# A third sum for the scatter-added expert blocks, and a loop unrolled by twelve

## The chip, the cores and the metric

The kernel runs on one core of one Trainium2 chip. A core has five engines with a queue of instructions each: TensorE (PE, matmuls; its weight loads are listed as PEld), VectorE (DVE), ScalarE (ACT), GpSimd (POOL) and SyncE (SP, which here issues DMAs). They run side by side and are tied together by semaphores. The metric is the device time of one execution in microseconds (us); lower is better.

## What is computed

One post-norm transformer layer in fp32 on 8 sequences of 512 tokens, width 256: attention with 16 heads, residual and layernorm; then a mixture of 16 experts of which each token takes 6, plus a shared expert, residual and layernorm.

```python
x = _layernorm(x + attn(x))                      # (8, 512, 256), causal
probs = softmax(xf @ gate_w.T); _, idx = top_k(probs + gate_b, 6)
cw = weights of the 6 chosen experts, 0 elsewhere
for each expert e:
    h = silu(xf @ W1.T + B1) * (xf @ W3.T + B3)
    y = y + cw[:, e:e+1] * (h @ W2.T + B2)       # each token gets 6 such terms
z = silu(xf @ ws1.T + bs1) * (xf @ ws3.T + bs3) @ ws2.T + bs2
out = _layernorm(x + y + z)
```

## The kernel before

The kernel works in three stages.

**Attention and routing (to about 530 us of the profile).** A loop over 8 sequences does attention, the first layernorm and the router. The normed tokens go to DRAM twice: as rows of `x1_d`, and, one copy for each chosen expert, by an indirect DMA of POOL into `xs_d`, where each expert's tokens stand together. Each row of `xs_d` carries its gates and its token number. At the end, tables say which expert each block of 128 rows belongs to.

**Blocks.** `BLOCKS` = 207 blocks of 128 rows go through their expert one after the other. For block k, SP loads the rows to `xb[k % 4]`; PE transposes them (L1029), ACT and DVE split them into a high and a low part (`xb_hi`, `xb_lo`), PE multiplies by the expert's first weights (bias L1038, product L1042), ACT and DVE make silu times gate (`hb`), PE transposes that (L1053), it is split again (`hb_hi`, `hb_lo`) and multiplied by the second weights (L1069). ACT weighs the result by the gate into `y_sb[k % 4]` (`weigh`, L1336), and POOL adds its 128 rows to a sum in DRAM by an indirect, accumulating DMA (`add_rows`, L2074). A token can be in any block, so two adds to the same sum must not be under way together. There are two sums: block k adds to `x1_d` where k is even and to `z_d` where it is odd, and waits on `added[k % 2]` until the add of block k - 2 has landed. `weigh` of block k waits for the add of block k - 4, whose `y_sb` buffer it overwrites, and the second product of block k + 2 waits for `y_out`, since PE has two PSUM banks for it.

The blocks are written out by `UNROLL` = 8: two turns straight (`LATE_TURNS`, in which the last four experts' weights still come in), 23 turns of a hardware loop, and a last one of 7. At the start of every turn PE reads the eight blocks' weight offsets from a table into registers, four to an instruction (L1079), and SP does the same for its rows.

**Shared expert and closing pass.** The shared expert runs in 48 tiles T (3 for each of 16 pieces of 256 tokens): PE `shared_up` (L781), ACT silu (`hidden`, L1297) and `h_hi`, DVE gate (L1799), low part `h_lo`, PE `shared_down` (L1010). 30 tiles run before the blocks and their results are stored to `z_d`; 18 run behind them. With the tiles from 36 on, the closing pass takes the 16 pieces m in the order `FINAL_ORDER`: SP loads `fin_x` from `x1_d` and `fin_z` from `z_d` (L720), POOL adds the two (`final_sum`, L2085, two pieces ahead), DVE adds the shared expert's result from PSUM for the last six pieces (L1862), takes the statistics (L1866, L1871), and after each of five groups of pieces POOL makes the inverse deviation (L2100), DVE the shift (L1883) and ACT normalizes (L1374). The L1862 of a piece frees the PSUM bank in which PE wants to start the next but one. Every engine's order here is the order in which the code is written: on POOL low part of tile T, inverse if due, sum of piece m + 2; on DVE gate of tile T, split of x1 if due, shift if due, statistics of piece m.

## Time and profile before

| | |
|---|---|
| device time, 3 runs | 1142.87 us median (1142.61 to 1143.4) |
| profiled execution | span 1184.2 us; no other time of it is recorded |
| blocks, third turn to last (666.88 to 1097.74 us) | 430.86 us for 184 blocks |
| last add to a sum issued | 1127.52 us |
| last matmul | about 1170.8 us |

| engine | busy us | share of the span |
|---|---|---|
| PE | 1050.3 | 89% |
| DVE | 754.6 | 64% |
| POOL | 736.1 | 62% |
| ACT | 672.2 | 57% |

In the timelines below a row has the start in us, the duration in us, engine, line and operation, result and operands, how many instructions were merged, and in brackets how long the engine had been idle before it and what ended that. "issue" is idle time in which the engine waited for nothing that the profile shows. Matmul ends are modelled.

### The profile page before, as it was taken

The numbers are of one execution on the slowest core, as the hardware profiler recorded it, in microseconds if no ns is written. First come the engines' busy times: TensorE is split into PE (matmuls) and PEld (weight loads), VectorE is DVE, ScalarE is ACT, GpSimd is POOL, SyncE is SP. The second block draws the span as 40 slices with busy tenths as digits, with TensorE's granted clock in tenths as the row PEclk, the third lists the DMA queues.
The fourth block names the chain that finished last, engine by engine and source line by source line (L and its number), as shares of the span: only waits on it lengthen the run. The fifth ranks groups of instructions, "written<-read, shape, count | busy, mean of one in ns | idle before, by whom it ended". The sixth has DMA issues, their size and how long they took to land.

```text
span 1184.2 us, 28306 instructions
## 1 busy us (share of the span) xinstructions
PE 1050.3 (89%) x8028; PEld 853.9 (72%) x8029; DVE 754.6 (64%) x2400; ACT 672.2 (57%) x1684; POOL 736.1 (62%) x668
## 2 busy tenths in 40 slices
PE   7899998989898987885297999999999999999974
PEld 4546555545465544575287899999999999999973
DVE  8777787868777777465265655555555555555456
ACT  3666666656566666543145655555555555555536
POOL 4224387877778788664403566666666666666666
PEclk8999999999999999687599999999999999999987
DMA  6713344444444455465426676777776666666684
GB/s 183 193 44 109 102 125 167 142 154 128 155 137 159 142 181 157 147 216 168 161 100 169 120 119 116 116 118 119 117 118 112 116 114 112 117 111 120 108 286 151
DMA packets 127036, 163.53 MB, mean 138 GB/s; under 512 B 18800, under 2 KB 107504, under 8 KB 126704
## 3 DMA queue, kind: packets, MB, share of 16 engines
q1 hardware_dynamic: 82240, 99.73, 29.7%
q0 software_dynamic: 39024, 54.29, 24.4%
q10 hardware_dynamic: 5696, 8.55, 2.2%
q8 instruction: 41, 0.67, 0.3%
q14 instruction: 35, 0.29, 0.1%
HBM read 65.36 MB, written 73.85 MB: 118 GB/s over the span
## 4 chain that ended last, share of the span: by engine, by line
PE 66%; DVE 12%; DMA 6%; ACT 4%; issue 4%; another core or an unknown queue 4%; POOL 1%; SPq 1%; ACTq 0%; DVEq 0%; POOLq 0%
PE psum L1042 15%; PE psum L1069 11%; PE psum L781 9%; PE psum L811 5%; PE psum L823 5%; PE psum L796 4%; PE psum L1029 4%; PE psum L1053 3%; DVE rowmax L1479 3%; PE psum L1038 3%; DMA z_d<-y_sb,tokens 2%; PE psum L798 2%; ACT probs L1142 2%; DMA xb<-xs_d 2%
## 5 line engine op out<-in xcount | busy, mean ns | idle before, releaser
L1142 ACT ACTIVATE probs<-psum 128x512 f32<-128x512 f32 (+2 forms) x384 | 187.0, 531 | 128.6 <-PE psum L811 114.0
L1479 DVE TENSOR_REDUCE rowmax<-psum 128x1 f32<-128x512 f32 (+3 forms) x352 | 212.7, 633 | 69.9 <-PE psum L798 62.8
L2000 POOL DMA_INDIRECT xs_d<-x1p,index x192 | 199.7, 1040 | 65.6 <-issue 43.2
L2074 POOL DMA_INDIRECT x_d<-y_sb,tokens x104 | 162.8, 1566 | 116.5 <-ACT y_sb L1336 90.4
L1818 DVE TENSOR_TENSOR xb_lo<-psum,xb_hi 128x256 fp32r<-128x256 f32 x207 | 87.7, 424 | 199.7 <-ACT xb_hi L1133 198.7
L2074 POOL DMA_INDIRECT z_d<-y_sb,tokens x103 | 160.8, 1561 | 86.7 <-ACT y_sb L1336 56.3
L1042 PE MATMUL psum<-we_hi_lo,xb_hi 128*128 x828 | 200.3, 323 | 0.0
L1336 ACT ACTIVATE y_sb<-psum,combine 128x256 f32<-128x256 f32 x207 | 98.3, 475 | 150.5 <-PE psum L1069 51.5
L1069 PE MATMUL psum<-we_hi_lo,hb_hi 88*128 (+1 forms) x828 | 174.2, 303 | 0.0
L796 PE MATMUL psum<-stack_k,stack_q 96*128 96x256 bf16 (+3 forms) x512 | 138.7, 310 | 11.6 <-issue 5.4
L1042 PEld LDWEIGHTS psum<-we_hi_lo,xb_hi 128*128 128x128 f32 x828 | 145.9, 189 | 0.0
L1942 POOL TENSOR_SCALAR_AFFINE_SELECT probs<-probs 128x512 f32<-128x512 f32 x128 | 85.7, 670 | 96.8 <-ACT probs L1142 93.8
L811 PE MATMUL psum<-stack_q,stack_k 99*128 99x256 bf16 (+3 forms) x512 | 118.6, 307 | 28.3 <-ACT probs L1142 16.9
L1042 PE MATMUL psum<-we_hi_lo,xb_lo 128*128 x414 | 134.1, 324 | 0.0
L1069 PEld LDWEIGHTS psum<-we_hi_lo,hb_hi 88*128 88x128 f32 (+1 forms) x828 | 125.6, 189 | 0.2 <-issue 0.2
L1069 PE MATMUL psum<-we_hi_lo,hb_lo 88*128 x414 | 116.2, 281 | 0.0
L823 PE MATMUL psum<-probs,values 128*32 128x512 f32 (+3 forms) x1024 | 95.0, 456 | 9.6 <-DVE attn L1556 7.2
L811 PEld LDWEIGHTS psum<-stack_q,stack_k 99*128 99x128 bf16 x512 | 40.4, 98 | 85.4 <-ACT probs L1142 49.9
L798 PE MATMUL psum<-causal,ident_bf 128*128 128x128 bf16 x512 | 101.2, 224 | 0.0
L1326 ACT ACTIVATE hb<-psum 128x176 f32<-128x176 f32 x207 | 65.7, 317 | 61.6 <-PE psum L1042 56.1
L781 PE MATMUL psum<-x1T,ws_hi_lo 128*128 128x256 f32 x576 | 86.2, 300 | 8.3 <-issue 6.3
L796 PEld LDWEIGHTS psum<-stack_k,stack_q 96*128 96x128 bf16 x512 | 50.4, 99 | 56.8 <-issue 27.4
(205 smaller groups left out, 2353.7 us busy)
## 6 DMA issues: line engine op xcount, KB each, us to landing
xb<-xs_d SPq DMA_DIRECT2D x207, 138.0 KB
stack_q<-q_h SPq DMA_DIRECT2D x48, 128.0 KB
stack_k<-k_h SPq DMA_DIRECT2D x45, 128.0 KB
w_raw<-in_we SPq DMA_DIRECT2D x9, 608.0 KB
xT_raw<-in_xT SPq DMA_DIRECT2D x9, 512.0 KB
stack_q<-q_m SPq DMA_DIRECT2D x32, 128.0 KB
stack_k<-k_m SPq DMA_DIRECT2D x32, 128.0 KB
x_res<-in_x SPq DMA_DIRECT2D x8, 512.0 KB
```

The source lines that it names most:

```text
L781: last = nc.tensor.matmul(dst, lhs(a, k), rhs(b, k), start=n == 0, stop=n == 3 * KD - 1)
L796: nc.tensor.matmul(dst, stack_q[par][0:STACK, head, qt * P:qt * P + P], stack_k[par][0:STACK, head, 0:width], start=True, stop=False)
L798: last = nc.tensor.matmul(dst[:, width - P:width], ident_bf[:], causal[:], start=False, stop=True)
L811: last = nc.tensor.matmul(st[f % ST_BANKS][:, i * width:(i + 1) * width], stack_k[par][0:STACK + SHIFT_ROWS, head, kt * P:kt * P + P], sta ...
L823: last = nc.tensor.matmul(ov[32 * j:32 * j + 32, kt * P:S], values[par][:, kt, GH * g + j, :], probs[kt][:, j, :], start=kt == 0, stop=kt ...
L1042: last = nc.tensor.matmul(uv, (xb_hi, xb_lo)[a][k % 2][:, d, :], w_flat[:, bass.ds(at + b * W_COLS + d * UP, UP)], start=False, stop=d == ...
L1069: last = nc.tensor.matmul(y, (hb_hi, hb_lo)[a][k % 2][0:rows, d, :], w_flat[0:rows, bass.ds(at + b * W_COLS + W2_AT + d * D, D)], start=d ...
L1142: nc.scalar.activation(probs[kt][:, heads[0]:heads[0] + n, :], st[f % ST_BANKS][:, 0:n * width].rearrange("p (h t) -> p h t", h=n), ACT.Ex ...
L1336: nc.scalar.activation(y_sb[k % 4][:], y_ps[k % 2][:, 0:D], ACT.Copy, scale=combine[:, k:k + 1]).then_inc(y_out, 1)
L1479: nc.vector.reduce_max(rowmax[gpar][:, heads[0]:heads[0] + n, qt], src, AX.X).then_inc(sm_free, 1)
L2000: nc.gpsimd.indirect_dma_start(out=xs_d[:, :], out_offset=bass.IndirectOffsetOnAxis(ap=index[tp][:, n:n + 1], axis=0), in_=x1p[tp][:, n // ...
L2074: nc.gpsimd.indirect_dma_start(out=(x1_d, z_d)[k % 2][:, :], out_offset=bass.IndirectOffsetOnAxis(ap=tokens[:, k:k + 1], axis=0), in_=y_sb ...
```

## The change

There is a third sum, `y_d`, in DRAM. It starts as zeros: at the head of each of the first seven turns of the attention loop SP writes a piece of up to 640 rows from a tile of zeros. Block k now adds to sum k % 3, and waits for the add of block k - 3. `weigh` still waits for the add of block k - 4, which is now the semaphore of another sum. The blocks are written out by 12: two turns straight (24 blocks), 15 of the loop, a last one of 3. In the closing pass SP loads a third tile `fin_y` for each piece, and DVE adds it to `fin_x` ahead of L1862 or the statistics.

```diff
-UNROLL = 8
+UNROLL = 12
+SUMS = 3
...
+            def set_third_sum(piece):
+                rows = y_d[Y_ROWS * piece:min(Y_ROWS * piece + Y_ROWS, T_ALL + P)]
+                sp.dma_start(rows.rearrange("(q p) d -> p q d", p=P),
+                             pad_block[:, 0:D].unsqueeze(1).to_broadcast([P, rows.shape[0] // P, D])).then_inc(y_set, 16)
...
+                if b < Y_PIECES:
+                    set_third_sum(b)
...
-            for n, src, dst in ((1, z_d, fin_z), (0, x1_d, fin_x)):
-                sp.wait_ge(added[n], 16 * ((BLOCKS + 1 - n) // 2))
+            for n, src, dst in ((0, x1_d, fin_x), (1, z_d, fin_z), (2, y_d, fin_y)):
+                sp.wait_ge(added[n], 16 * ((BLOCKS + SUMS - 1 - n) // SUMS))
...
             for i in FINAL_ORDER[FINAL_FIRST:]:
                 load_final(i, x1_d, fin_x)
                 load_final(i, z_d, fin_z)
+                load_final(i, y_d, fin_y)
...
                 if not (early and k < 4):
-                    act.wait_ge(added[k % 2], 8 * j0 + 16 * (k // 2 - 1))
+                    act.wait_ge(added[(k - 4) % SUMS], adds + 16 * ((k - 4) // SUMS + 1))
...
                 dve.wait_ge(fin_sum, m + 1)
+                dve.wait_ge(fin_third_loaded[i], 16)
+                nc.vector.tensor_tensor(fin_x[i][:], fin_x[i][:], fin_y[i][:], ALU.add).then_inc(fin_third, 1)
+                dve.wait_ge(fin_third, m + 1)
...
                 nc.gpsimd.indirect_dma_start(
-                    out=(x1_d, z_d)[k % 2][:, :], out_offset=bass.IndirectOffsetOnAxis(ap=tokens[:, k:k + 1], axis=0),
-                    in_=y_sb[k % 4][:], in_offset=None, compute_op=ALU.add).then_inc(added[k % 2], 16)
+                    out=(x1_d, z_d, y_d)[k % SUMS][:, :], out_offset=bass.IndirectOffsetOnAxis(ap=tokens[:, k:k + 1], axis=0),
+                    in_=y_sb[k % 4][:], in_offset=None, compute_op=ALU.add).then_inc(added[k % SUMS], 16)
```

On PE, at the head of the loop over turns, there stood before (`tables` holds the offsets; `select` is the bias product of the turn's first block):

```order
L557 UNCONDITIONAL_BRANCH
L557 ISA
L1079 TENSOR_LOAD tables
L1079 ISA
L1079 TENSOR_LOAD tables
L1036 REGISTER_ALU
L1037 REGISTER_ALU
```

and now, with the lines of the changed file:

```order
L564 UNCONDITIONAL_BRANCH
L564 ISA
L1104 TENSOR_LOAD tables
L1104 ISA
L1104 TENSOR_LOAD tables
L1104 ISA
L1104 TENSOR_LOAD tables
L1061 REGISTER_ALU
L1062 REGISTER_ALU
```

Three loads of offsets stand ahead of the first matmul of a turn in place of two; the loop's body goes from 200 printed rows to 295.

On DVE, the statistics of the first piece in `FINAL_ORDER` (one of the last six), before:

```order
L1862 TENSOR_TENSOR fin_x<-psum,fin_x 128x512 [waits down_done,fin_sum]
L1866 BN_STATS fin_stats<-fin_x 128x6 [waits z_done]
L1866 BN_STATS fin_stats<-fin_x 128x6
L1871 BN_AGGR fin_mv<-fin_stats 128x2 [waits fin_stats_done]
L1871 BN_AGGR fin_mv<-fin_stats 128x2
```

and now:

```order
L1891 TENSOR_TENSOR fin_x<-fin_x,fin_y 128x512 [waits fin_third_loaded10,fin_sum]
L1895 TENSOR_TENSOR fin_x<-psum,fin_x 128x512 [waits down_done,fin_third]
L1899 BN_STATS fin_stats<-fin_x 128x6 [waits z_done]
L1899 BN_STATS fin_stats<-fin_x 128x6
L1904 BN_AGGR fin_mv<-fin_stats 128x2 [waits fin_stats_done]
L1904 BN_AGGR fin_mv<-fin_stats 128x2
```

An addition of two SBUF tiles stands ahead of each of the 16 pieces' statistics; POOL's own list there is the same as before.

## Rows read from the trace of the kernel before

**Rows 1.** Busy time by stretch: each engine, clock, DMA share, GB/s.

```profile
685.40:907.90 222.50, 222.38 (x1634) 216.99 (x1633) 129.47 (x577) 130.47 (x384) 148.80 (x96) 1.00 0.71 117
907.90:1097.74 189.84, 186.71 (x1362) 181.09 (x1361) 100.86 (x481) 105.49 (x320) 124.56 (x80) 1.00 0.65 115
```

**Rows 2.** PE timeline, first matmul of a block (L1038), turn starting at 815.31.

```profile
815.31 0.42 PE L1038 MATMUL psum<-we_hi_lo,select 98*128 x1
817.70 0.33 PE L1038 MATMUL psum<-we_hi_lo,select 98*128 x1
...
829.17 0.33 PE L1038 MATMUL psum<-we_hi_lo,select 98*128 x1
```

**Rows 3.** The same: second turn, entry of the loop, a later turn, last turn.

```profile
643.51 0.42 PE L1038 MATMUL psum<-we_hi_lo,select 98*128 x1 [0.42 <-issue]
...
666.88 0.42 PE L1038 MATMUL psum<-we_hi_lo,select 98*128 x1 [0.86 <-issue]
...
946.15 0.42 PE L1038 MATMUL psum<-we_hi_lo,select 98*128 x1 [0.38 <-issue]
...
1097.74 0.42 PE L1038 MATMUL psum<-we_hi_lo,select 98*128 x1
```

**Rows 4.** PE's sequencer at the start of a turn, 812 to 816.

```profile
L1079 PEldq TENSOR_LOAD <-tables x2: 333/362/392, 814.1 to 814.6; - x2
L557 PEldq COMPARE_BRANCH  x1: 215/215/215, 813.6 to 813.6; - x1
```

**Rows 5.** The same, 943 to 947.

```profile
L557 PEldq COMPARE_BRANCH  x1: 215/215/215, 944.5 to 944.5; - x1
```

**Rows 6.** Waits of ACT, 940 to 1080: total us, times, longest.

```profile
ACT y_sb L1336 <- DMA z_d<-y_sb,tokens: 24.5, 26, 1.2
```

**Rows 7.** POOL timeline behind the blocks; x2 merges two operations.

```profile
1127.52 1.57 POOL L2074 DMA_INDIRECT x_d<-y_sb,tokens  x1 [2.10 <-issue]
1132.11 0.74 POOL L2046 TENSOR_TENSOR h_lo<-hidden,h_hi 128x256 fp32r<-128x256 f32 x1 [3.02 <-ACT h_hi L1133]
1135.34 2.48 POOL L2085 TENSOR_TENSOR fin_x<-fin_x,fin_z 128x512 f32<-128x512 f32 x2 [2.50 <-DMA fin_x<-x_d]
1138.58 1.27 POOL L2085 TENSOR_TENSOR fin_x<-fin_x,fin_z 128x512 f32<-128x512 f32 x1 [0.75 <-DMA fin_z<-z_d]
1139.81 1.18 POOL L2046 TENSOR_TENSOR h_lo<-hidden,h_hi 128x256 fp32r<-128x256 f32 x1
```

**Rows 8.** DVE timeline behind the blocks.

```profile
1126.14 0.69 DVE L1472 TENSOR_TENSOR x1T<-x1T_late,x1T 128x512 fp32r<-128x512 f32 x1
...
1136.64 0.69 DVE L1862 TENSOR_TENSOR fin_x<-psum,fin_x 128x512 f32<-128x512 f32 x1 [6.23 <-POOL fin_x L2085]
...
1138.79 1.61 DVE L1472 TENSOR_TENSOR x1T<-x1T_late,x1T 128x512 fp32r<-128x512 f32 x1
...
1143.93 0.48 DVE L1799 SCALAR_TENSOR_TENSOR hidden<-psum,bias,hidden 128x256 f32<-128x256 f32 x1 [0.66 <-ACT hidden L1297]
...
1147.28 0.77 DVE L1472 TENSOR_TENSOR x1T<-x1T_late,x1T 128x512 fp32r<-128x512 f32 x1 [0.38 <-ACT x1T L1133]
...
1151.57 1.25 DVE L1883 SCALAR_TENSOR_TENSOR fin_shift<-fin_mv,fin_rstd 128x8 f32<-128x8 f32 x1 [2.09 <-POOL fin_rstd L2100]
...
1156.31 1.00 DVE L1472 TENSOR_TENSOR x1T<-x1T_late,x1T 128x512 fp32r<-128x512 f32 x1
...
1162.48 1.25 DVE L1883 SCALAR_TENSOR_TENSOR fin_shift<-fin_mv,fin_rstd 128x8 f32<-128x8 f32 x1 [1.48 <-POOL fin_rstd L2100]
...
1171.93 1.22 DVE L1883 SCALAR_TENSOR_TENSOR fin_shift<-fin_mv,fin_rstd 128x8 f32<-128x8 f32 x1 [1.07 <-POOL fin_rstd L2100]
...
1178.82 0.16 DVE L1883 SCALAR_TENSOR_TENSOR fin_shift<-fin_mv,fin_rstd 128x4 f32<-128x4 f32 x1 [1.12 <-POOL fin_rstd L2100]
```

**Rows 9.** Busy time by stretch as in rows 1: the closing pass.

```profile
1135.00:1177.00 42.00, 26.49 (x180) 24.82 (x180) 31.66 (x90) 20.85 (x46) 34.73 (x31) 0.81 0.66 242
```

**Rows 10.** PE timeline: the gap ahead of tile 36's second product.

```profile
1137.48 0.77 PE L1010 MATMUL psum<-ws_hi_lo,h_hi 128*128 128x256 f32 x2 [4.12 <-DVE fin_x L1862]
```

More of the change, by code:

```diff
@@ L171 @@
 LATE_CHECK = 4
-assert all((e - (E - TOP_K)) * T_ALL >= P * UNROLL * (LATE_TURNS + 1) for e in W_ORDER[W_FRONT - ST:])
+assert all((e - (E - TOP_K)) * T_ALL >= P * (UNROLL * LATE_TURNS + LATE_CHECK) for e in W_ORDER[W_FRONT - ST:])
 AFTER_SCORES, AFTER_ATTEND, AFTER_ROUTER, AFTER_RANK, AFTER_TABLES, AFTER_SCATTER = 2, 5, 9, 12, 13, 15
@@ L254, in postln_layer @@
         z_d = nc.dram_tensor("z_d", (T_ALL + P, D), fp32).ap()
+        y_d = nc.dram_tensor("y_d", (T_ALL + P, D), fp32).ap()
         x1T_d = nc.dram_tensor("x1T_d", (B, P, KD, S), fp32).ap()
@@ L379, in postln_layer @@
         fin_z = [sb(f"fin_z{n}", [P, HALF, D]) for n in range(HALVES)]
+        fin_y = [sb(f"fin_y{n}", [P, HALF, D]) for n in range(HALVES)]
         x1T_late = [sb(f"x1T_late{n}", [P, KD, HT_TOK]) for n in range(HALVES - HC1 - 2)]
@@ L490, in postln_layer @@
         y_out = sem("y_out")
-        added = [sem(f"added{n}") for n in range(2)]
+        added = [sem(f"added{n}") for n in range(SUMS)]
+        y_set = sem("y_set")
         fin_loaded = [sem(f"fin_loaded{n}") for n in range(HALVES)]
+        fin_third_loaded = [sem(f"fin_third_loaded{n}") for n in range(HALVES)]
         fin_sum = sem("fin_sum")
-        fin_y = sem("fin_y")
+        fin_third = sem("fin_third")
         fin_stats_done = sem("fin_stats_done")
@@ L559, in by_blocks, with adds_by_turns @@
             body(BLOCKS - LAST_BLOCKS, False, True)
+        def adds_by_turns(eng, body):
+            a_turn = 16 * (UNROLL // SUMS)
+            for turn in range(LATE_TURNS):
+                body(UNROLL * turn, a_turn * turn, turn == 0, False)
+            with eng.Fori(0, BLOCKS // UNROLL - LATE_TURNS) as turn:
+                body(UNROLL * turn + LATE_TURNS * UNROLL, a_turn * turn + a_turn * LATE_TURNS, False, False)
+            body(BLOCKS - LAST_BLOCKS, a_turn * (BLOCKS // UNROLL), False, True)
         def blocks_of(last):
@@ L1326, in block_silu, with weigh @@
                 nc.scalar.activation(hb[k % 2][:], uv_ps[k % 2][:, 0:H], ACT.Silu).then_inc(silu_done, 1)
-            def weigh(j0, k, early):
+            def weigh(j0, k, adds, early):
                 act.wait_ge(y_full, j0 + (k + 1))
@@ L1356, in split_late_w, with weigh_before, blocks @@
                         late_w_hi, 1)
-            def blocks(j0, first, last):
+            def weigh_before(j0, adds, k, early):
+                turns = k // UNROLL
+                weigh(*moved(j0, k), adds + 16 * (UNROLL // SUMS) * turns, early)
+            def blocks(j0, adds, first, last):
                 for k in range(blocks_of(last)):
@@ L1362, in blocks @@
                     if not (first and k < 3):
-                        weigh(*moved(j0, k - 3), first)
+                        weigh_before(j0, adds, k - 3, first)
                     if not (last and k == LAST_BLOCKS - 1):
@@ L1428, in _ @@
             high_x(0, 0, True)
-            by_blocks(act, blocks)
+            adds_by_turns(act, blocks)
             end, k = BLOCKS - LAST_BLOCKS, LAST_BLOCKS - 1
+            adds = 16 * (end // SUMS)
             high_h(end, k - 1, False)
-            weigh(end, k - 2, False)
+            weigh(end, k - 2, adds, False)
             act.wait_ge(late_w_lo, 2 * LATE_W)
@@ L1435, in _ @@
             high_h(end, k, False)
-            weigh(end, k - 1, False)
+            weigh(end, k - 1, adds, False)
             silu(T1 + 1)
@@ L1439, in _ @@
             split_x1(HC1 + 1)
-            weigh(end, k, False)
+            weigh(end, k, adds, False)
             for T in range(T1 + 2, T_SH):
@@ L2061, in bias_rows, with add_rows, blocks @@
                                             channel_multiplier=-1).then_inc(hb_ones, 1)
-            def add_rows(j0, k, early):
+            def add_rows(j0, k, adds, early):
                 pool.wait_ge(y_out, j0 + (k + 1))
-                if not (early and k < 2):
-                    pool.wait_ge(added[k % 2], 8 * j0 + 16 * (k // 2))
+                if not (early and k < SUMS):
+                    pool.wait_ge(added[k % SUMS], adds + 16 * (k // SUMS))
                 elif k == 0:
+                    pool.wait_ge(x1_stored, STORED * (B + 1))
+                    pool.wait_ge(z_set, 32)
+                elif k == 1:
                     for n in range(2):
                         pool.wait_ge(z_stored[n], 16 * (HC1 // 2))
-                    pool.wait_ge(z_set, 32)
                 else:
-                    pool.wait_ge(x1_stored, STORED * (B + 1))
+                    pool.wait_ge(y_set, 16 * Y_PIECES)
                 settle(pool, passed_pool)
                 nc.gpsimd.indirect_dma_start(
-                    out=(x1_d, z_d)[k % 2][:, :], out_offset=bass.IndirectOffsetOnAxis(ap=tokens[:, k:k + 1], axis=0),
-                    in_=y_sb[k % 4][:], in_offset=None, compute_op=ALU.add).then_inc(added[k % 2], 16)
-            def blocks(j0, first, last):
+                    out=(x1_d, z_d, y_d)[k % SUMS][:, :], out_offset=bass.IndirectOffsetOnAxis(ap=tokens[:, k:k + 1], axis=0),
+                    in_=y_sb[k % 4][:], in_offset=None, compute_op=ALU.add).then_inc(added[k % SUMS], 16)
+            def blocks(j0, adds, first, last):
                 for k in range(blocks_of(last)):
-                    add_rows(j0, k, first)
+                    add_rows(j0, k, adds, first)
             def final_sum(m):
@@ L2093, in _ @@
             bias_rows()
-            by_blocks(pool, blocks)
+            adds_by_turns(pool, blocks)
             def final_inverse(k):
```

5 lines of the change are left out of this document (4 added, 1 removed).

## The prediction

> **What bounds the kernel now.** I read the busy time by stretch first, then PE's timeline through the blocks, the waits of ACT, and last the chain of waits and the timelines behind the blocks. Attention is left nearly as it is, so two stages matter.
>
> In the blocks PE is the bound: it is busy 222.38 of 222.50 us in the first half and 186.71 of 189.84 in the second [rows 1]. A block takes 2.294 us (817.70 to 829.17 is five of them [rows 2]). What is lost is lost where one turn of the loop meets the next. Eight blocks would need 18.35 us. The first half is twelve turns in 222.50 us, 18.54 each: 0.19 us lost at a seam. The second is ten turns in 189.84 us, 18.98 each: 0.63 lost. The reader should see why in the sequencer's rows: branch, two loads of offsets, first matmul take the same 1.7 us at both seams (813.6 to 815.31, 944.5 to 946.15 [rows 2 to 5]); in the second half the sequencer reaches the branch half a microsecond nearer to the matmuls that it has already queued. What makes it late there: ACT's weighing waits for adds, 26 times in 140 us for those to `z_d` alone, 24.5 us together [rows 6]; the sequencer waits for that weighing before a second product. So the two sums cost 0.44 us per turn, in ten turns of 23. From 666.88 to 1097.74 it is 430.86 us for 184 blocks; 184 x 2.294 = 422.1, so all seams together cost 8.8 us.
>
> Behind the blocks nobody is full, and DVE and POOL share the bound: 31.66 and 34.73 of 42 us busy [rows 9], with each waiting for the other by turns, and the last shift on DVE at 1178.82 starts the end of ACT's work and the last store [rows 8].
>
> **The adds' wait (removed).** With three sums an add has the time of three blocks, 6.9 us, in which to land. That ACT waits with two sums, 4.6 us, shows that landing plus POOL's issue is about that long; 6.9 is enough. The ten seams of 0.63 go back to 0.19 as far as this cause goes. If nothing else changed, the loop would lose 23 x 0.19 = 4.4 us in place of 8.8.
>
> **Unrolling by twelve (seams).** There are 15 loop turns in place of 23, but each begins with three loads of offsets in place of two (front, the order on PE). Loads are 0.33 to 0.39 us each and stand in sequence with an instruction between them [rows 4, 5]; I price the third at 0.45. Is it hidden? At the good seams the queued matmuls already run out just before the first matmul of the new turn comes, since 0.19 is lost there. So the lead of the sequencer is used up by two loads, and a third is exposed: a seam costs 0.19 + 0.45 = 0.64 us. 15 x 0.64 = 9.6 us for blocks 24 to 203, against 8.8 before: +0.8. Ahead of the loop's turns there are two more turn starts, at 643.51 and at the loop's entry at 666.88, with 0.42 and 0.86 us of idle time [rows 3]. They come again at blocks 12 and 24 with a third load each: +0.9. Blocks together: +1.7 us. The bounds: if the third load is hidden by a longer lead, 15 x 0.19 - 8.8 = -5.9; if each seam is as bad as the second half's with 0.45 on top, 15 x 1.08 - 8.8 + 0.9 = +8.3. I take +1.7, being nearest to the rows of a seam without add waits.
>
> **Zeroing the third sum.** Seven DMAs of up to 640 rows on SP, at the head of an attention turn, behind the shift rows and ahead of the next input. What is queued behind them is loaded long before its use; attention is bound by PE, ACT and DVE among themselves. I take 0, with +4 as the upper bound (half a microsecond of SP's issue for each, exposed).
>
> **Swapped waits of the first adds** name things that finished earlier: 0.
>
> **The end of the adds.** The last add is now issued at 1127.52, 2.10 us idle before it, after PE is long done with the blocks [rows 7]; it will come some 7 us earlier, since it no longer waits for the one two before. But that is mostly given away. POOL's list has the low part of tile 36 ahead of the first sum; that ran at 1132.11 and was waiting for ACT, not for a load [rows 7]. The first sum can follow at 1132.85 in place of 1135.34, and ends at 1134.1 (1.24 each). Then DVE must add the third tile. POOL starts its second sum at the same moment; if it goes first, DVE gets its turn at 1135.35 and L1862 stands at 1136.04 in place of 1136.64: 0.6 us gained [rows 8]. PE's gap of 4.12 us [rows 10] shrinks by just that. The third load per piece (16 x 256 KB more) is spread over a stretch in which DMA is at two thirds [rows 9] and begins 7 us earlier; it isn't late.
>
> **The third additions (added).** 16 of them, one ahead of L1862 already counted, 15 to go. The shape is that of L1472: two SBUF inputs, 128x512 fp32. This takes 0.69 us with POOL idle (1126.14) and 1.61, 0.77 and 1.00 in the three cases beside POOL, mean 1.13 [rows 8]. That it is POOL's work that delays it shows in the pair 1138.79 and POOL's 1139.81: DVE's addition is long while POOL's sum runs from 1138.58 to 1139.85, and then POOL's low part takes 1.18 where it takes 0.74 [rows 7, 8]. The shifts, of 8 elements a partition, take 1.25 beside POOL and 0.16 without. POOL is busy for 34.73 us of 42 [rows 9]; over a stretch some 9 us longer that is 0.68. So 0.68 x 1.13 + 0.32 x 0.69 = 0.99, with 0.03 of step 1.02, and 15 of them are 15.3 us.
>
> The Trainium skill (SBUF — State Buffer, Who interferes with whom) states that a DVE instruction with two SBUF inputs contends with a GpSimd instruction that reads SBUF, and that who issues second waits for the whole of the other. The trace agrees as far as the pair above goes. An estimate by that page, that no collision escapes and costs half of a sum of 1.27: 15 x (0.72 + 0.68 x 0.64) = 17.3 us in place of 15.3; the sum here goes by the rows.
>
> Against this stand DVE's idle times in the stretch, which a later DVE no longer has: 0.66, 0.38, 2.09, 1.48 and 1.07, 5.7 us [rows 8]. POOL's inverses are ready by then, for POOL's own list hasn't grown. 15.3 - 5.7 - 0.6 = +9.0 us. Lower bound: no collisions at all: 15 x 0.72 = 10.8, less 5.7, less 1.8 (L1862 at 1134.85) = +3.3. Upper bound: 15 x 1.64, less 6.3, that is +18. I take +9.0. All of it moves the last shift and with it the end; ACT's last normalizations and the store hang on it as before.
>
> **Sum.** +1.7 + 0 + 9.0 = +10.7 us on the profiled execution of 1184.2 us. Its span is 41.3 us over the median of the runs; nothing in the profile says where these lie, so I carry the difference over in microseconds: 1142.87 + 10.7 = 1153.6 us.
>
> **Rivals.**
> 1. Faster: PE's sequencer gets more lead. With no wait on adds ahead of a second product, the lead at the branch grows by at least the 0.45 us of the third load, and seams cost 0.19 again: -5.9 us. For it: seams in the second half show how the lead moves with ACT's waits [rows 4, 5]. Against it: in the first half there were hardly such waits, and the lead was still used up. It decides the sign only if the closing pass costs less than 5.9 us; with its lower bound, +3.3, the time is 1142.87 - 2.6 = 1140.3.
> 2. The same lead, but the closing pass as forecast: 1142.87 - 5.9 + 9.0 = 1146.0.
> 3. The longer body of PE's loop no longer stays on the chip and is fetched in each turn. Before, the idle time at the loop's entry, where code is new, is 0.86 us against 0.38 at later seams [rows 3]; some 0.5 us more in each of 15 turns is +7.5: 1161.1. The Trainium skill (Runtime: NRT & Kernel Launch, Instruction fetch mechanics) says that a taken branch whose target isn't in the current window of two pages stalls on a fetch, and gives PE room for 2048 instructions; by the window a body of 295 printed rows (more, as each matmul brings a weight load) could fall out of it, by the room it would not. No row here shows such a fetch within the loop.
> 4. The change doesn't do what it says: three adds under way slow each other so that ACT still waits. The loop's seams then cost 15 x (0.63 + 0.45) = 16.2 us in place of the 9.6 forecast, and the time is 1160.2. Against it: 6.9 us is much against a landing of about 4.
>
> **How the numbers follow.** Forecast 0.65; rival 1 0.12; rival 2 0.12; rival 3 0.06; rival 4 0.02; 0.03 for a time near the old one by a mixture. About 0.2% (2.3 us) is what a measurement can tell from no change. Faster: rival 1, 0.12. Same: the mixture and the lower edge of rival 2, 0.08. Slower: 0.80. The forecast's own range is 1147 to 1159 from the bounds of the additions and seams; rival 2 is inside the range when it goes down to 1142, and rival 1 and the far parts of 3 and 4 are left out: 1142 to 1160.
>
> **What would show it.** In the profile after: no wait of `y_sb` on a DMA; PE seams of 0.5 to 0.7 us in every turn, with three loads of offsets at each (0.2 would be rivals 1 and 2, over 1.0 rivals 3 or 4); instruction fetches among the DMA queues between 700 and 1100 us for rival 3. The last add issued some 7 us earlier relative to the last block. Third additions with a mean near 1.0 us (near 0.7: the lower bound), DVE busy for over 45 us of the closing pass with its waits for `fin_rstd` gone, and 9 us more from the first L1862 to the last shift. The forecast is wrong if the closing pass is not longer by at least 5 us.

## The result and the profile after

The changed kernel takes 1148.38 us, median of 9 runs (1145.58 to 1153.66), beside 1139.87 us for the kernel before on the same chip (9 runs, 1135.26 to 1143.40). The ratio is 1.0067, 95% interval 1.0041 to 1.0093: slower, by 7.6 us (4.7 to 10.6); the two medians stand 8.5 us apart. Forecast were 10.7 us more. Run again on another chip it was 1.0102 (1.0053 to 1.0151).

The head of the page after (busy us, share of the span, number of instructions):

```profile
span 1151.9 us, 28124 instructions
PE 1046.9 (91%) x8028; PEld 853.1 (74%) x8029; DVE 774.4 (67%) x2416; ACT 676.1 (59%) x1684; POOL 746.6 (65%) x668
```

DVE has 19.8 us more work than before and POOL 10.5 (against a second execution of before 19.5 and 6.0); PE and ACT are within 4 us of what they had. The waits of ACT through the blocks (us in total, times, longest), which answer to [rows 6]:

```profile
ACT y_sb L1361 <- PE psum L1094: 110.2, 192, 2.1
ACT hb L1351 <- PE psum L1067: 79.8, 195, 1.2
```

There is no wait for an add any more. PE's timeline, the first matmul of five of the turns, which answers to [rows 2, 3]:

```profile
648.21 0.43 PE L1063 MATMUL psum<-we_hi_lo,select 98*128 x1 [0.35 <-issue]
...
704.52 0.43 PE L1063 MATMUL psum<-we_hi_lo,select 98*128 x1 [0.58 <-issue]
...
732.65 0.42 PE L1063 MATMUL psum<-we_hi_lo,select 98*128 x1 [0.55 <-issue]
...
760.74 0.42 PE L1063 MATMUL psum<-we_hi_lo,select 98*128 x1 [0.55 <-issue]
...
1042.65 0.43 PE L1063 MATMUL psum<-we_hi_lo,select 98*128 x1 [0.47 <-issue]
```

From 704.52 to 1042.65 it is 338.13 us for twelve turns, 28.18 each: twelve blocks of 2.294 and 0.65 us of seam. Single turns hardly differ, but the changed kernel's own blocks are shorter than 2.294 us (see the experiment with the loads spread), so this 0.65 is not the whole seam. Now the closing pass: groups of its instructions from 1093 to 1148 us (busy us, mean ns of one | idle before, what ended it).

```profile
L2120 POOL TENSOR_TENSOR fin_x<-fin_x,fin_z 128x512 f32<-128x512 f32 x16 | 22.2, 1393 | 0.0
L1891 DVE TENSOR_TENSOR fin_x<-fin_x,fin_y 128x512 f32<-128x512 f32 x16 | 13.1, 817 | 3.7 <-POOL fin_x L2120 3.7
L2079 POOL TENSOR_TENSOR h_lo<-hidden,h_hi 128x256 fp32r<-128x256 f32 x12 | 11.1, 926 | 17.9 <-ACT h_hi L1158 17.9
```

The third additions have a mean of 0.82 us, not 0.99. Twelve of the 16 take 0.68 to 0.70 us, the other four 0.90, 0.96, 1.28 and 1.73. The same two POOL groups before, from 1131 to 1181 us:

```profile
L2085 POOL TENSOR_TENSOR fin_x<-fin_x,fin_z 128x512 f32<-128x512 f32 x16 | 20.8, 1306 | 3.3 <-DMA fin_x<-x_d 2.5 <-DMA fin_z<-z_d 0.8
L2046 POOL TENSOR_TENSOR h_lo<-hidden,h_hi 128x256 fp32r<-128x256 f32 x12 | 9.4, 785 | 7.6 <-ACT h_hi L1133 7.5
```

POOL's sums became 0.09 us longer each and its low parts 0.14, 3.1 us together: part of the collisions between DVE and POOL are paid there. And POOL's 3.3 us of waiting for loads (1.9 in the second execution of before) are gone.

The stages of several profiled executions, in us. "Attention" is the time up to the first block; "seams" is blocks 24 to 203 less 180 x 2.294, for every kernel alike; "to first" and "to last" run from the end of the last block's second product to the first addition of a psum tile and to the last shift (of before 1118.83, 1136.64 and 1178.82 [rows 8]; the kernels of the lower rows are described below).

| execution | attention | blocks 0 to 23 | seams | to first | to last | third addition, mean |
|---|---|---|---|---|---|---|
| before | 623.51 | 61.89 | 9.12 | 17.81 | 59.99 | |
| before, again | 577.14 | 64.49 | 9.50 | 16.32 | 59.26 | |
| after | 582.46 | 65.75 | 8.90 | 16.91 | 65.25 | 0.82 |
| after, again | 578.19 | 64.46 | 8.34 | 16.91 | 64.84 | 0.85 |
| unrolling alone | 576.94 | 65.04 | 21.09 | 17.49 | 60.57 | |
| zeroing alone | 578.73 | 64.67 | 8.29 | 18.49 | 60.54 | |
| zeroing and closing pass | 580.40 | 61.30 | 6.90 | 18.65 | 67.29 | 0.84 |
| third addition left out | 575.22 | 63.72 | 8.43 | 15.14 | 55.09 | |
| two sums, loads spread | 576.69 | 64.27 | 7.07 | 17.69 | 60.92 | |
| three sums, loads spread | 582.71 | 64.59 | -3.72 | 16.90 | 65.69 | 0.89 |
| the same, again | 584.24 | 60.60 | -3.73 | 16.91 | 65.25 | 0.82 |
| additions three pieces ahead | 577.28 | 61.53 | -3.72 | 16.86 | 65.34 | 0.89 |
| the same, again | 583.70 | 61.42 | -3.72 | 16.80 | 65.26 | 0.87 |
| additions two pieces ahead | 576.70 | 61.15 | -3.72 | 15.45 | 66.75 | 0.69 |

The 41 us by which the profiled execution of before stood over its median were in attention, and the second execution does not have them. From the means of two executions each: blocks 0 to 23 +1.9, blocks 24 to 203 -0.7, closing pass +5.4; the last three blocks, which are in no column, are 0.4 us shorter. That is +6.2 us, beside 7.6 by the times. The +1.9 is not clear of the scatter: two executions of three sums with loads spread differ by 4.0 us in blocks 0 to 23.

### The profile page after: what moved, and what is told of

Same layout as the page of the kernel before. It is cut to its first block, busy times and chain, and to the rows that moved or that the text cites. A ratio compares the mean times of both kernels' runs of the same rounds, so it can differ in the third digit from the quotient of the medians.

```text
span 1151.9 us, 28124 instructions
## 1 busy us (share of the span) xinstructions
PE 1046.9 (91%) x8028; PEld 853.1 (74%) x8029; DVE 774.4 (67%) x2416; ACT 676.1 (59%) x1684; POOL 746.6 (65%) x668
## 4 chain that ended last, share of the span: by engine, by line
PE 71%; DVE 13%; ACT 5%; issue 5%; DMA 4%; POOL 1%; SPq 0%; ACTq 0%; POOLq 0%; DVEq 0%
PE psum L1067 17%; PE psum L1094 13%; PE psum L806 10%; PE psum L848 5%; PE psum L836 5%; PE psum L821 5%; PE psum L1054 4%; PE psum L1078 4%; DVE rowmax L1509 3%; PE psum L1063 3%; ACT probs L1167 2%; DMA xb<-xs_d 2%; PE psum L823 2%; PE psum L880 1%; PE psum L1035 1%
## 5 line engine op out<-in xcount | busy, mean ns | idle before, releaser
L2033 POOL DMA_INDIRECT xs_d<-x1p,index x192 | 203.9, 1062 | 54.7 <-issue 41.8
L2109 POOL DMA_INDIRECT x_d<-y_sb,tokens x69 | 107.9, 1564 | 82.5 <-ACT y_sb L1361 42.1
L2109 POOL DMA_INDIRECT z_d<-y_sb,tokens x69 | 108.0, 1565 | 65.3 <-ACT y_sb L1361 53.9
L2109 POOL DMA_INDIRECT y_d<-y_sb,tokens x69 | 107.9, 1564 | 50.3 <-issue 44.8
```

Source lines behind the costliest of these rows:

```text
L2033: nc.gpsimd.indirect_dma_start(out=xs_d[:, :], out_offset=bass.IndirectOffsetOnAxis(ap=index[tp][:, n:n + 1], axis=0), in_=x1p[tp][:, n // ...
L2109: nc.gpsimd.indirect_dma_start(out=(x1_d, z_d, y_d)[k % SUMS][:, :], out_offset=bass.IndirectOffsetOnAxis(ap=tokens[:, k:k + 1], axis=0), ...
```

## The experiments

Ratios are to the kernel before on the same chip at the same time, with 95% intervals.

**Unrolling alone** (u12_two_sums): two sums, twelve blocks in a turn.

```
-UNROLL = 8
+UNROLL = 12
```

> The kernel before with UNROLL = 12 alone: two sums, closing pass and attention as they were. Theory (a third load of offsets is exposed at every seam): seams in the loop cost 0.6 to 0.7 us where adds do not hold ACT and up to 1.1 where they do, 15 of them, so 9.6 to 16 us in place of 8.8; time +1 to +6 us against before. Rival (the third load is hidden and the seam cost counts turns only): 15 x 0.19 to 15 x 0.63, time -6 to 0 us.

Measured: 1145.28 us, ratio 1.0029 (0.9994 to 1.0063). The profiled execution, at 1155.12 us the longest of its twelve (1134.58 to 1155.12), lost 21.09 us at seams, and ACT waited for adds throughout. ACT's waits from 620 to 1090 us:

```profile
ACT y_sb L1336 <- DMA z_d<-y_sb,tokens: 75.0, 69, 2.1
ACT y_sb L1336 <- PE psum L1069: 45.0, 76, 0.7
ACT y_sb L1336 <- DMA x_d<-y_sb,tokens: 40.8, 46, 1.6
```

In this one execution late adds and three loads of offsets add up to more than the 9.6 to 16 us expected: 21.09 us over fifteen turns, where the third sum leaves 8.3 to 8.9. How much of it the median execution has, 10 us shorter, stays open; none of the others has a trace. The time alone, +3 us with an interval from -0.7 to +7, doesn't tell this kernel from before.

**Zeroing alone** (zero_only): the kernel before, with the seven fills of the third array and SP's wait for them, and no use of it.

```
+                if b < Y_PIECES:
+                    set_third_sum(b)
...
+                sp.wait_ge(y_set, 16 * Y_PIECES)
```

> The kernel before, with the seven DMAs that zero a third tensor in the attention turns; nothing adds to it or reads it. Theory (these DMAs are hidden): within 1 us of before, first block at the same time. Rival (they push back the loads behind them in attention, and part of the measured loss is there): +2 to +4 us, all of it ahead of the first block.

Measured: 1142.87 us, ratio 1.0034 (0.9999 to 1.0068), which is 0 to 8 us; the stages behind attention are those of before. The interval doesn't tell 0 from 4 us. Attention leans to a cost: in the ten profiled executions with the fills the first block comes at 575.2 to 584.2 us, mean 580.0; in three of the four without them it comes at 576.7 to 577.1 (the fourth is the one at 623.51). The scatter of attention told of below is larger than that difference, so a cost of some 3 us is not shown, and neither is 0.

**Zeroing and closing pass** (closing_only): the above, and the third array is loaded and added behind the blocks, while the blocks still go to two sums in turns of eight.

```
+                dve.wait_ge(fin_third_loaded[i], 16)
+                nc.vector.tensor_tensor(fin_x[i][:], fin_x[i][:], fin_y[i][:], ALU.add).then_inc(fin_third, 1)
+                dve.wait_ge(fin_third, m + 1)
```

> The kernel before with two sums and turns of eight, plus the zeroed third tensor, its 16 loads and the 16 third additions of DVE in the closing pass. Theory (the closing pass on DVE is the main cost): from the last second product of a block to the last shift 6 to 9 us longer than before's 60.0, time +6 to +9 us. Rival (the longer closing pass shows only because the adds end earlier, or the loss is in the blocks): under +3 us.

Measured: 1148.09 us, ratio 1.0075 (1.0048 to 1.0102), +9 us; closing pass 67.29 us, 7.3 to 8.0 over the two executions of before, as the theory had it. This alone is as slow as the whole change.

**Third addition left out** (three_no_dve_add): the changed kernel without the 16 additions, so the third sum is missing from the output; zeroing, loads and unrolling stay.

```
                 dve.wait_ge(fin_third_loaded[i], 16)
-                nc.vector.tensor_tensor(fin_x[i][:], fin_x[i][:], fin_y[i][:], ALU.add).then_inc(fin_third, 1)
-                dve.wait_ge(fin_third, m + 1)
```

> The changed kernel without the 16 additions of the third sum on DVE (zeroing, adds in rotation, turns of twelve and loads of the third tile stay; a third of the blocks' results is left out of the output). Theory: the closing pass from the last second product to the last shift falls from 65.3 us to 58 or 59, below before's 60.0 since the adds end earlier; time 6 to 7 us below the changed kernel, within 2 us of before. Rival (the loads, not the additions, lengthen the closing pass): it stays above 63 us and the time within 2 us of the changed kernel.

Measured: 1136.27 us, ratio 0.9986 (0.9959 to 1.0014): no slower than before. The closing pass is 55.09 us, so the additions cost 9.8 to 10.2 us, and without them the pass is 4.2 to 4.9 us shorter than before, for the adds end sooner. Both effects are larger than expected: the pass was to fall to 58 or 59 us, and the time to be 6 to 7 us under the changed kernel's, where the two ratios to before lie 0.8% apart, some 9 us. DVE's sixteen additions cost as much as the whole change loses, or more; what is left of the change without them, zeroing and third loads included, is not told from before.

**Before, again** (before_again).

> The kernel before once more, for a second trace of it: the first block came at 623.5 us in its first trace and at 575 to 582 us in five other traces, with the blocks and the closing pass of the usual length. If that was a matter of one execution, the first block comes at 575 to 585 us here, the seams from block 24 to 204 cost 7 to 9 us, and last second product to last shift is 60 to 61 us. If the change itself shortens attention, it comes at 615 us or later.

Measured: 1142.0 us, one run, span 1140.2 us. The first block comes at 577.14 us, so the 623.51 was a matter of one execution; the seams, 9.50 us, are a little over the expected 7 to 9, and the closing pass, 59.26 us, a little under the expected 60 to 61.

**Loads of offsets spread** (two_spread, and three_spread on the changed kernel). In each turn PE's sequencer reads the offsets of four blocks when it comes to them, not those of the whole turn at its head. One load stays at the head, for the first four blocks.

```
-                for q in range(0, UNROLL, 4):
-                    ats += nc.values_load_multi_w_load_instructions(
-                        offsets[0:1, bass.ds(j0 + q, 4)], engines=[mybir.EngineType.PE], ...
...
                 for k in range(count):
+                    if k % 4 == 0:
+                        ats += nc.values_load_multi_w_load_instructions(
+                            offsets[0:1, bass.ds(j0 + k, 4)], engines=[mybir.EngineType.PE], ...
```

> The kernel before, with PE's offsets loaded four at a time ahead of the block that first needs them (one load at the head of a turn, one in its middle) in place of two at the head. Theory (what a seam costs is the loads at the head, beyond the sequencer's lead): seams where adds do not hold ACT go from 0.2 to 0, those where they do from 0.6 to 0.2 or less; 184 blocks lose 1 to 4 us in place of 7 to 9, time -3 to -7 us. Rival (a seam costs the branch; or each load costs as much wherever it stands): 7 to 9 us as before, time within 2 us.

> The changed kernel with the same edit: one load at the head of a turn of twelve and two inside it. Theory: seams of 0.64 to 0.75 us fall to 0 to 0.2; blocks 24 to 204 lose 0 to 3 us in place of 8.9, time 6 to 9 us below the changed kernel, thus about that of before, since the longer closing pass (65 us in place of 60) stays. Rival (each load costs 0.45 us wherever it stands): 8 to 9 us lost, time as the changed kernel's.

Measured: 1139.16 us with two sums, ratio 0.9981 (0.9951 to 1.0011), and 1137.07 us with three, ratio 0.9944 (0.9916 to 0.9972). With two sums the theory missed: 7.07 us are still lost where 1 to 4 were expected, and the time is not told from that of before. With three sums it gained more than was expected: 0.9944 against the 1.0067 of the changed kernel on another chip, some 14 us where 6 to 9 were expected. PE passes from turn to turn without a seam there. PE's timeline of three_spread, first matmuls of blocks 22 to 25, the third of them the first of a turn:

```profile
642.75 0.32 PE L1063 MATMUL psum<-we_hi_lo,select 98*128 x1
645.02 0.32 PE L1063 MATMUL psum<-we_hi_lo,select 98*128 x1
647.30 0.32 PE L1063 MATMUL psum<-we_hi_lo,select 98*128 x1
649.57 0.32 PE L1063 MATMUL psum<-we_hi_lo,select 98*128 x1
```

and the same place between two turns of the changed kernel:

```profile
732.65 0.42 PE L1063 MATMUL psum<-we_hi_lo,select 98*128 x1 [0.55 <-issue]
...
735.02 0.32 PE L1063 MATMUL psum<-we_hi_lo,select 98*128 x1
737.30 0.32 PE L1063 MATMUL psum<-we_hi_lo,select 98*128 x1
```

Every block takes 2.273 us here, the first of a turn too. In the changed kernel the blocks in the middle of a turn take 2.27 to 2.29. Measured by 2.273, a seam of the changed kernel costs 28.18 - 27.28 = 0.90 us. The sequencer's instructions at a turn of the changed kernel, of the line that reads the offsets in 730 to 734 us, and of the branch in 700 to 706 us (least, median and greatest ns, first and last start):

```profile
L1104 PEldq TENSOR_LOAD <-tables x3: 329/332/427, 730.9 to 732.0; - x3
...
L564 PEldq COMPARE_BRANCH  x1: 220/220/220, 702.2 to 702.2; - x1
```

The last load has ended by 732.4, 0.2 us or more before the matmul that stood behind it. From the branch at 702.2 to that turn's first matmul at 704.52 it is 2.3 us, where it was 1.7 with two loads [rows 2, 4]: the third load takes about 0.55. In three_spread, 699 to 703 us, the branch is followed by one load,

```profile
L1108 PEldq TENSOR_LOAD <-tables x1: 398/398/398, 700.8 to 700.8; - x1
```

which has ended by 701.2, and the turn's first matmul starts at 701.86, one block of 2.273 us behind the last. A single load at the head is hidden.

With two sums it goes in two parts. The first twelve turns of the loop (640.96 to 861.12 us) take 18.35 us each and have no seam; first matmuls of three blocks of two_spread, the third of them the first of a turn:

```profile
654.72 0.33 PE L1038 MATMUL psum<-we_hi_lo,select 98*128 x1
657.01 0.33 PE L1038 MATMUL psum<-we_hi_lo,select 98*128 x1
659.31 0.33 PE L1038 MATMUL psum<-we_hi_lo,select 98*128 x1
```

So 2.294 us is the bare block of the kernels with eight blocks in a turn, and 2.273 that of the twelve-block kernels at their best, whether they have two sums or three. Why they differ by 0.02 us is open. The -3.72 us of three_spread in the table is this difference, 180 times; by its own block its seams cost 0.06 us. The later turns of two_spread take 18.80 to 19.18 us, 0.5 to 0.8 over, and there ACT waits for adds; between 641 and 861 us it doesn't. ACT's waits from 620 to 1070 us:

```profile
ACT y_sb L1337 <- PE psum L1069: 58.2, 101, 0.6
ACT y_sb L1337 <- DMA z_d<-y_sb,tokens: 52.1, 45, 1.9
ACT y_sb L1337 <- DMA x_d<-y_sb,tokens: 43.0, 44, 2.3
```

So the two edits are worth more together than apart: against before's 9.1 to 9.5 us, the third sum with twelve blocks leaves 8.3 to 8.9, the spread loads alone 7.07, both -3.72. The step from 7.07 to -3.72 is not the third sum's alone, since the turns also go from eight blocks to twelve; three sums in turns of eight, or two sums in turns of twelve with the loads spread, were not run.

**Additions three pieces ahead** (three_ahead): on top of three_spread, DVE adds the third tile into `fin_z`, three pieces before the piece that it finishes, and POOL's sum waits for it. **Three_spread and the changed kernel again** ran beside it.

```
+            def final_third(m):
+                i = FINAL_ORDER[m]
+                dve.wait_ge(fin_loaded[i], 32)
+                dve.wait_ge(fin_third_loaded[i], 16)
+                nc.vector.tensor_tensor(fin_z[i][:], fin_z[i][:], fin_y[i][:], ALU.add).then_inc(fin_third, 1)
...
+                if m == 0:
+                    for ahead in range(3):
+                        final_third(ahead)
                 if m >= 0:
                     final_stats(m)
+                    if m + 3 < HALVES:
+                        final_third(m + 3)
...
+                pool.wait_ge(fin_third, m + 1)
```

> The changed kernel with PE's offsets read four at a time inside the turn (as in three_spread), and VectorE's sixteen third additions moved three pieces ahead: fin_y goes into fin_z before GpSimd adds fin_z to fin_x, so no third addition stands between GpSimd's sum and the first psum addition any more. Theory (the closing pass costs what its sixteen additions take on VectorE, and only the idle ones in front of the first psum addition can be hidden): the first psum addition comes 1.7 to 2.6 us earlier after the last block than in three_spread (14.3 to 15.2 instead of 16.9 us), the stretch from the last block to the last shift is 62 to 64 us instead of 65.7, and the time is 2 to 3 us under three_spread's. Rival (the closing pass is bound by the two engines together, so that an addition costs the same wherever it stands; or GpSimd now waits for VectorE once per piece): the stretch stays at 65 to 68 us and the time is within 1 us of three_spread's or above it.

> The same kernel as three_spread, beside three_ahead on one chip, so that the two are compared there. Theory: 0.4 to 0.7 per cent under the kernel before, as it was (0.9944), 4.5 to 8 us; no seam in the blocks, and the stretch from the last block to the last shift at 65 to 66 us. Rival (its lead was that chip's): within 0.2 per cent of the kernel before.

> The changed kernel as it is, on the same chip as three_spread, so that the price of its seams is read there. Theory: 0.5 to 0.8 per cent over the kernel before (6 to 9 us), and 11 to 13 us over three_spread, of which 9 to 12 us are between the 24th and the 204th block. Rival (the difference of three_spread lies elsewhere than in the seams): under 6 us between the two, or the blocks alike.

Measured: three_ahead 1132.77 us, ratio 0.9957 (0.9932 to 0.9982); three_spread 1133.19 us, 0.9963 (0.9931 to 0.9996); the changed kernel 1149.80 us, 1.0102 (1.0053 to 1.0151). The rival came out: three_ahead is within 1 us of three_spread, and the first psum addition came no sooner. DVE's timeline of three_ahead:

```profile
1071.04 1.39 DVE L1892 TENSOR_TENSOR fin_z<-fin_z,fin_y 128x512 f32<-128x512 f32 x2 [0.52 <-DMA fin_y<-y_d]
1074.71 1.29 DVE L1892 TENSOR_TENSOR fin_z<-fin_z,fin_y 128x512 f32<-128x512 f32 x1 [2.29 <-DMA fin_y<-y_d]
1075.93 0.68 DVE L1899 TENSOR_TENSOR fin_x<-psum,fin_x 128x512 f32<-128x512 f32 x1
```

Its third addition waited for a load issued 4.7 us earlier, and the psum addition stood behind it. Between three_spread and the changed kernel lie here 16.6 us of median where 11 to 13 were expected. The two profiled executions are 9.5 us apart: 12.1 us in blocks 24 to 203, as expected, and 3.9 in the blocks before, against 6.0 the other way in attention, which nothing in the edit explains.

**Additions two pieces ahead** (three_ahead2), and three_ahead again beside it.

```
-                    for ahead in range(3):
+                    for ahead in range(2):
...
-                    if m + 3 < HALVES:
-                        final_third(m + 3)
+                    if m + 2 < HALVES:
+                        final_third(m + 2)
```

> As three_ahead, with the third additions two pieces ahead instead of three. In three_ahead the third of the three additions in front of the first psum addition waited 2.29 us for its piece of y_d, which SyncE had issued only 4.73 us before, and the first psum addition stood behind it, at 16.86 us after the last block as before. With two ahead nothing waits there: VectorE's two additions end at 1.7 us before that point, GpSimd's first sum at about 15.2 us after the last block. Theory: the first psum addition at 15.2 to 15.5 us, and, if the closing pass is bound by VectorE's row from there, the last shift 1.5 us earlier than three_ahead's 65.34, at 63.5 to 64.2 us; the time 1 to 2 us under three_ahead's, too little for its interval. Rival (from the second piece on the pass is paced by GpSimd and the loads, or by both engines together): the first psum addition comes earlier and the last shift still falls at 65.0 to 65.7 us.

> The same kernel as three_ahead, beside three_ahead2 on one chip. Theory: as it was, 0.3 to 0.6 per cent under the kernel before; first psum addition at 16.9 us and last shift at 65.3 us after the last block. Rival (its lead was that chip's): within 0.2 per cent of the kernel before.

Measured: 1135.04 us, ratio 0.9976 (0.9948 to 1.0004), and three_ahead 1136.63 us, 0.9995 (0.9967 to 1.0022). The first psum addition does come 1.4 us sooner, at 15.45 us, and the last shift falls at 66.75 us, later than with three. The additions are shorter here (0.69 us of mean), and POOL waits for them, 9.8 us in all. Groups of three_ahead2 from 1045 to 1140 us:

```profile
L2130 POOL TENSOR_TENSOR fin_x<-fin_x,fin_z 128x512 f32<-128x512 f32 x16 | 20.8, 1303 | 9.8 <-DVE fin_z L1892 9.8
L1892 DVE TENSOR_TENSOR fin_z<-fin_z,fin_y 128x512 f32<-128x512 f32 x16 | 11.0, 693 | 0.8 <-DMA fin_y<-y_d 0.8
```

The rival, with its 65.0 to 65.7 us, comes nearest to what happened, and even it was too low. An addition costs about the same wherever it stands on DVE: with it moved, POOL waits for DVE in place of DVE for POOL. For three_ahead its own rival came out here, a time within 0.2% of before's; its 0.9957 of the other chip did not return. Three sums with the loads spread is the version that was faster than before on both chips on which it ran, by 5.6 and 3.7 thousandths; it was not run on this one, so a lead of that size is shown for two chips only. Moving the additions adds nothing that can be measured.

## Why the prediction was right, and where it was off

**Sign and size.** Slower by 7.6 us where 10.7 were forecast; the median is 1148.38 us where 1153.6 stood, inside the range. Of the 5.2 us between them 3.0 are that before itself came out at 1139.87 us beside it, in place of 1142.87. In the sum, the closing pass was too dear by 3.6 us: +5.4 by the stages where +9.0 was forecast. The prediction had called itself wrong if that pass was not longer by 5 us, so it passed its own mark narrowly.

**The adds' wait.** Right: no wait of `y_sb` on a DMA is left, where there had been 26 for `z_d` alone [rows 6].

**Seams.** The size came out: 0.65 us in every turn where 0.64 was forecast, and for fifteen turns 8.3 to 8.9 us where 9.6 was, beside 9.1 to 9.5 before. That it is so near is partly luck, for two errors cancel. Against the changed kernel's own block a seam is 0.90 us, 0.71 more than the 0.19 of before, where the third load was priced at 0.45; the load takes 0.55 of it, and 0.16 is open. And twelve blocks of 2.273 us take 0.25 less than twelve of 2.294, which the prediction didn't have. Counted so, the third sum with twelve blocks in a turn won nothing at the seams: they cost 12.1 to 12.7 us in place of 9.1 to 9.5, and shorter blocks, 3.8 us, more than hide it. The argument itself, that two loads use up the sequencer's lead and a third is exposed whole, holds: where no add holds ACT, the seam is gone with one load at the head, 0.19 us with two, and 0.90 with three. Rivals 1 and 2 (the lead grows, a seam costs 0.19) fall by the 0.65, and 4 (adds still wait) by the missing waits. For the two turn starts ahead of the loop's turns 0.9 us was forecast; blocks 0 to 23 took 1.9 us more, within their scatter, so this term is neither confirmed nor refuted.

**Instruction fetches** (rival 3). None: between 700 and 1000 us the changed kernel's DMA queues are two, and the instruction queues, which carry 80 packets over the whole execution, are not among them.

```profile
q0 software_dynamic: 18367, 16.74, 49.4%
q1 hardware_dynamic: 18411, 18.07, 23.2%
```

The Trainium skill (Runtime: NRT & Kernel Launch, Instruction fetch mechanics) has a window of two pages, by which a taken branch to a target outside it stalls, and room for 2048 instructions on PE. The trace has no fetch in a loop of twelve blocks, 204 matmuls and as many weight loads a turn, which fits the room; whether that body is larger than the window it doesn't show.

**The end of the adds.** The step had the time right and only the half of its worth that lies in front. POOL's timeline of the changed kernel:

```profile
1082.87 1.56 POOL L2109 DMA_INDIRECT y_d<-y_sb,tokens  x1 [1.05 <-ACT y_sb L1361]
...
1094.23 0.74 POOL L2079 TENSOR_TENSOR h_lo<-hidden,h_hi 128x256 fp32r<-128x256 f32 x1 [9.79 <-ACT h_hi L1158]
1094.93 4.17 POOL L2120 TENSOR_TENSOR fin_x<-fin_x,fin_z 128x512 f32<-128x512 f32 x3
```

The last add is issued 1.8 us after the last product ends, 6.9 us sooner than before (1127.52 against 1118.83 [rows 7]; 6.1 by the second execution of before), and the low part comes first and waits for ACT, as forecast. In front of the first psum addition the step was right within the scatter of before. Without the third additions that addition comes 1.2 to 2.7 us sooner than before, and the prediction had POOL's first sum 2.5 us sooner; with them it stands at 16.91 us, 0.9 sooner than in one execution of before and 0.6 later than in the other, where 0.6 sooner was forecast. What the step lacked is the stretch behind: without the third additions it is 39.95 us in place of 42.18 and 42.94, 2.2 to 3.0 shorter, and POOL no longer waits for loads there. With the additions, zeroing-and-closing-pass against the changed kernel gives 2.0 to 2.5 us for the earlier end (67.29 against 65.25 and 64.84), where 0.6 was kept in the sum.

**The third additions.** The mis-sized term. DVE's timeline of the changed kernel:

```profile
1096.23 1.73 DVE L1891 TENSOR_TENSOR fin_x<-fin_x,fin_y 128x512 f32<-128x512 f32 x1 [3.70 <-POOL fin_x L2120]
1098.00 0.69 DVE L1895 TENSOR_TENSOR fin_x<-psum,fin_x 128x512 f32<-128x512 f32 x1
...
1110.06 0.68 DVE L1891 TENSOR_TENSOR fin_x<-fin_x,fin_y 128x512 f32<-128x512 f32 x1
...
1113.00 1.25 DVE L1916 SCALAR_TENSOR_TENSOR fin_shift<-fin_mv,fin_rstd 128x8 f32<-128x8 f32 x1 [0.70 <-POOL fin_rstd L2135]
...
1126.28 1.25 DVE L1916 SCALAR_TENSOR_TENSOR fin_shift<-fin_mv,fin_rstd 128x8 f32<-128x8 f32 x1 [0.75 <-POOL fin_rstd L2135]
...
1137.73 0.92 DVE L1916 SCALAR_TENSOR_TENSOR fin_shift<-fin_mv,fin_rstd 128x8 f32<-128x8 f32 x1
...
1146.34 0.16 DVE L1916 SCALAR_TENSOR_TENSOR fin_shift<-fin_mv,fin_rstd 128x4 f32<-128x4 f32 x1 [1.12 <-POOL fin_rstd L2135]
```

From the first psum addition to the last shift it is 48.34 us (1098.00 to 1146.34) where it was 42.18: +6.2, forecast +9.6 (+5.0 by the second execution of each). The first addition, of 1.73 us, stands ahead of this stretch. The fifteen inside it take 11.35 us, 0.76 each; with 0.03 of step that is 11.8 in place of 15.3, and this is the whole miss. The price took 0.68 of the additions to be slowed by POOL, at 1.13 us; three of these fifteen were. In most of the others POOL's instruction started with DVE's or behind it, and where the two then overlapped for long it was POOL's that became longer. What the stretch absorbed came out, 5.6 us where 5.7 was forecast: DVE's idle time in it fell by 4.0 us, from 10.0 to 6.0, its other instructions became 1.2 shorter, and the 0.4 left is the step, which the trace doesn't show apart. Of the three waits for `fin_rstd` that were to go, 2.09, 1.48 and 1.07, the third went and the others shrank to 0.70 and 0.75; the last one, 1.12, stayed. POOL's inverses were not ready by then; that this comes of POOL's own instructions having become longer fits their 3.1 us, but no run tests it. DVE's busy time from 1093 to 1148 us missed its mark of 45 narrowly:

```profile
1093.00:1148.00 55.00, 30.54 (x201) 28.38 (x199) 44.25 (x110) 26.78 (x57) 40.36 (x33) 0.79 0.71 262
```

(Columns: stretch, length, busy us and number for PE, PEld, DVE, ACT and POOL, granted clock, share of the DMA engines, GB/s.) The estimate by the Trainium skill's page SBUF — State Buffer (Who interferes with whom), 17.3 us for the additions, was farther off than the rows' 15.3. Its rule that the second to issue waits is seen in both directions: DVE's first addition, started 0.07 us behind a sum of POOL, takes 1.73, where one with POOL idle (at 1142.41) takes 0.69; and POOL's low part takes 0.74 with DVE's addition not beside it and 1.27 when both start at 1110.06, while DVE's then takes 0.68. The 0.53 us that the low part loses is less than the whole of DVE's addition, for which the page has it wait.

```profile
1110.06 1.27 POOL L2079 TENSOR_TENSOR h_lo<-hidden,h_hi 128x256 fp32r<-128x256 f32 x1 [0.94 <-ACT h_hi L1158]
```

**Zeroing.** Taken at 0 with 4 as the bound. The variant with the fills alone has 0 to 8 us and medians 3.8 apart, so this term is the least certain of the sum, and 0 is not shown.

## What to carry to other kernels

A third accumulator buys time in which an add can land, and is paid in the closing pass with one more addition per tile, on engines that may be full there: compare the two stretches, not the wait alone. Register loads at the head of an unrolled loop use up the lead of a sequencer, so a longer body does not help if it brings its loads with it; put each load where its value is first needed, a few blocks into the turn. Here that paid only once the adds no longer held ACT: with two sums it gave nothing that can be told from noise. To see what a seam costs, measure it against a block of the same kernel: the unit may change with the edit, as here from 2.294 to 2.273 us, and 180 of them are 3.8 us.

## What the runs showed of the hardware

The same kernel has executions 6 us apart that differ in the clock granted in the last part of attention, before the first block. Two executions of three_ahead, 1131.72 and 1137.96 us, from 400 to 500 us (columns as above):

```profile
400.00:500.00 100.00, 84.67 (x699) 52.59 (x698) 69.75 (x183) 62.24 (x134) 80.42 (x82) 0.91 0.51 166
```

```profile
400.00:500.00 100.00, 86.13 (x668) 51.67 (x667) 67.42 (x175) 61.33 (x132) 77.39 (x82) 0.85 0.49 161
```

In the first, PE did 699 matmuls at a mean clock of 0.91, in the second 668 at 0.85; from 500 to 577 us the clock is 0.96 and 0.89, and the first block starts at 577.28 and 583.70 us. In 100 to 400 us both had 1.00. Why the clock falls lower in some executions is open. Over the twelve runs of three_spread 0.01 of a run's mean clock goes with 7.8 us, at a correlation of -0.89; in u12_two_sums the correlation is only -0.20, so the clock is not the only thing that varies. Hence intervals of three thousandths even with twelve runs, and hence stages were compared here; the closing pass repeats within 0.8 us, blocks 0 to 23 only within 4.

One more was not expected: the third load per piece slows the other two. Loads behind the blocks, 1075 to 1150 us of the changed kernel (number, KB each, median us from issue to landing), and the same of before, 1113 to 1188 us:

```profile
fin_x<-x_d SPq DMA_DIRECT2D x16, 256.0 KB, 7.1
fin_z<-z_d SPq DMA_DIRECT2D x16, 256.0 KB, 7.9
fin_y<-y_d SPq DMA_DIRECT2D x16, 256.0 KB, 8.2
```

```profile
fin_z<-z_d SPq DMA_DIRECT2D x16, 256.0 KB, 6.4
fin_x<-x_d SPq DMA_DIRECT2D x16, 256.0 KB, 6.0
```

The second execution of each has 6.7 and 7.7 us in place of 6.1 and 6.5. In the changed kernel neither DVE nor POOL waits for a load behind the blocks. What is moved to the very front of the pass meets them first: in three_ahead DVE waited 0.52 and 2.29 us for pieces of the third sum.
